# Transformer block with patch tokens, attention over one big row set and a top-2 mixture of experts: the feed-forward part and the elementwise work around it rebuilt

## The chip, the cores and the metric

The kernel runs on one core of one Trainium2 chip. The metric is device time in microseconds for one execution; lower is better. The core has a matrix engine (TensorE, PE in the profile, whose weight loads are PEld), a vector engine (VectorE, DVE), a scalar engine (ScalarE, ACT), a third elementwise engine (GpSimd, POOL) and a queue engine for transfers (SyncE, SP). Matmul results land in PSUM, eight banks of 128 x 512 fp32; GpSimd works on SBUF alone.

## The reference

Input `x` is (8, 64, 128, 64) fp32: batch, channels, time, variables. Each of 8 x 64 series is cut into 16 patches of 16 steps, Fourier-transformed and projected to 64 features, which gives 8192 tokens of 64 features. Then:

```python
f = l2norm(h)                                  # 8192 x 64
attn = softmax(f @ f.T)                        # 8192 x 8192
h = layernorm(h + l2norm(0.8 * f + 0.2 * attn @ f))
logits = h @ router_w.T                        # 8 experts, best 2, weights renormalised
out = h
for e in range(8):
    out = out + combine[:, e:e+1] * (gelu(h @ w1[e] + b1[e]) @ w2[e] + b2[e])
result = layernorm(h + out)
```

## The kernel before

Tokens sit 128 to a tile (`NT` = 64 tiles), and eight tiles make a group (`G` = 8, `NG` = 8 groups), kept in `h` as 128 x 64 tiles x 64 features. Every engine runs an order written out by hand; semaphores tie them together, and each engine takes its own instructions strictly in that order.

1. Up to about 86 us, `x` is loaded in eight pieces of 1 MB per half (three slots in `ring`), multiplied by folded weights (`product`, L368, fp32) and transposed into token tiles (`tokens`, L402, fp32 transposes with 64 rows, the two halves of the array in turn).
2. Attention takes 512 steps `s`: 8 blocks of 1024 queries (`QC`) times 64 key tiles. A step is three fp16 products (`scores`, L431), one exponential on ScalarE (L709, with the row sum as accumulator), one subtraction on VectorE that forms the low part of the probabilities (`low_part`, L794), and the products with the values (`high_sums` L446, `low_sums` L459). Meanwhile GpSimd splits the expert weights into three bf16 parts (L273 to L277, into `wp`).
3. In the last query block, `beside(t)` puts work for the first groups between the steps: `attention_tokens` (L469), `attended` (L815, L818), squares and sums, the scaled residual, mean and variance of the first normalisation, `token_transposes` (L481) and the routing of group 0.
4. The feed-forward loop then runs over 8 groups `g`, with eight slots `s` each. A slot is one pair of experts for 512 tokens: `u = 8 * g + s`, with `n = u // 4` the half group and `i = u % 4` the pair of experts. `up(u)` (L509) makes three matmuls of 512 columns, one for each part in `wp`, against fp16 `hT`, whose 128 rows are the high and the low half of the 64 features. ScalarE applies the activation with the bias (L724). `expand(u)` (L569) spreads the routing weights from 16 rows to 128 rows, `weigh` (L912) multiplies the two on VectorE, `down` (L580) adds two experts' products into bank 4 by its column halves in fp32, and three more matmuls (L586) add the bias `b2`. After each half group bank 4 is copied (L732), transposed back by four fp32 transposes (L596), and added to `h` (L918, L919).

In the same slots the engines work for later groups: `attention_tokens(g + 4)`, `attended(g + 3)` and its norm, the first normalisation of `g + 2` (mean L831, centring on GpSimd L288, squares L667, variance L836, power L280, scaling L841, `high_half` L671, low half on GpSimd L304, transposes L481), the routing of `g + 1` (`logits_out` L863, L864 and `route`, fifteen small instructions from L872 to L905 on 128 x 64 values, then `combine_transposes` L500 and `combine_out` L681), and the second normalisation of `g - 1` (mean L831, centring on GpSimd L348, squares L743, variance L836, power L280, scaling on GpSimd L345), whose result goes out by two DMAs. `up(u)` waits for the activation of `u - 2` and `expand(u)` for `weigh(u - 2)`: banks 0 and 1, and banks 2 and 3, take turns.

GpSimd's order in a group (`elementwise(x, y, q, z)` with x = g + 3, y = g + 2, q = g + 1, z = g - 1), which decides what queues behind what: centre y, power for z - 1, power for the norm of x, power for y, exponential of q, low half of y, residual of x, scale z - 1, centre z. Each of these waits for its own semaphore, so a late one holds up all behind it.

## Time and profile before

| | |
|---|---|
| median of 3 runs | 964.14 us (962.71 to 968.96) |
| profiled execution, own time | 968.87 us |
| its span | 967.1 us, 31034 instructions |
| PE busy | 908.5 us (94%) |
| DVE busy | 801.7 us (83%) |
| ACT busy | 646.4 us (67%) |
| POOL busy | 164.4 us (17%) |
| mean granted TensorE clock | 0.984 of full speed |
| DMA | 26.19 MB, mean 27 GB/s |

Busy time is the union of an engine's instructions. A busy matrix engine is not one at its peak, since matmuls overlap. An fp32 matmul that is no transpose stands in the trace as two MATMUL instructions (128 for the 64 in `down` and 128 for the 64 in `product`). The mean duration of an instruction includes its fill and drain, so that two instructions without a dependence start closer together than their durations say.

### The profile page before, as it was taken

To read this page: it belongs to the slowest core of one execution; us is meant where nothing else is said; L and a number is where in the kernel's file an instruction comes from. 1 tells how busy PE (TensorE), PEld (TensorE's weight loads), DVE (VectorE), ACT (ScalarE), POOL (GpSimd) and SP (SyncE) were. 2 spreads that over 40 slices of the span, in tenths; PEclk is the share of its full clock that TensorE was granted. 3 is DMA by queue.
4 is the path that set the end of the run, shared out by engine and by line. 5 is a ranking of instruction groups with operands and counts; after the bars stand their busy time and mean duration, and the time that the engine had idled before them with its cause. 6 is when DMAs were issued, how large, how long until landed. Compare 5 with 4: busy or idle time off the path is not lost.

```text
span 967.1 us, 31034 instructions
## 1 busy us (share of the span) xinstructions
PE 908.5 (94%) x13562; PEld 547.0 (57%) x13562; DVE 801.7 (83%) x923; ACT 646.4 (67%) x1179; POOL 164.4 (17%) x129
## 2 busy tenths in 40 slices
PE   4987799999999999999999999999998799999895
PEld 2433455566866776786678666666654454333231
DVE  6134998898898889889888988888898898999673
ACT  0223768788778878887777888788766665555352
POOL 3043800000000000000000000000024513466433
PEclk9999999999999999999999999999999999999798
DMA  9695400000000000000000000000000000000001
GB/s 301 193 233 113 79 2 2 2 3 3 2 3 3 2 3 2 3 2 3 2 3 2 3 2 2 3 2 3 2 2 2 1 2 2 1 12 12 12 23 33
DMA packets 28486, 26.19 MB, mean 27 GB/s; under 512 B 9552, under 2 KB 26064, under 8 KB 28352
## 3 DMA queue, kind: packets, MB, share of 16 engines
q1 hardware_dynamic: 19408, 14.98, 6.8%
q10 hardware_dynamic: 8496, 8.57, 3.3%
q8 instruction: 107, 1.75, 0.8%
q0 software_dynamic: 448, 0.67, 0.3%
q14 instruction: 27, 0.22, 0.1%
HBM read 17.92 MB, written 2.10 MB: 21 GB/s over the span
## 4 chain that ended last, share of the span: by engine, by line
PE 81%; DVE 9%; DMA 3%; issue 3%; POOL 2%; ACT 1%; SPq 0%; POOLq 0%; ACTq 0%; DVEq 0%
PE ps L431 31%; PE ps L446 22%; PE ps L459 11%; PE ps L368 5%; DVE ring L794 4%; PE ps L509 3%; DMA ring<-in_x_dram 3%; PE ps L580 3%; PE ps L569 2%; POOL stat L280 1%; PE ps L469 1%; DVE ring L912 1%; PE ps L586 1%; ACT combT L681 1%; PE ps L596 1%
## 5 line engine op out<-in xcount | busy, mean ns | idle before, releaser
L794 DVE TENSOR_TENSOR ring<-ring 128x1024 f16<-128x1024 f32 x512 | 614.1, 1248 | 50.1 <-ACT ring L709 49.1
L709 ACT ACTIVATE ring<-ps 128x1024 f32<-128x1024 f32 x512 | 519.2, 1020 | 145.0 <-PE ps L431 144.9
L431 PE MATMUL ps<-big 64*64 64x512 f16 x6144 | 384.9, 377 | 2.8 <-DVE h L774 2.6
L431 PEld LDWEIGHTS ps<-big 64*64 64x64 f16 x6144 | 225.0, 106 | 115.8 <-DVE h L774 3.0
L446 PE MATMUL ps<-ring,fs 64*64 64x512 bf16 x4096 | 285.4, 387 | 1.6 <-ACT ring L709 0.7
L446 PEld LDWEIGHTS ps<-ring,fs 64*64 64x64 f16 x4096 | 151.0, 106 | 79.3 <-issue 5.3
L459 PE MATMUL ps<-ring,fs 64*64 64x512 f16 x2048 | 163.2, 379 | 16.5 <-DVE ring L794 15.9
L280 POOL TENSOR_TENSOR stat<-stat,cst 128x8 f32<-128x8 f32 x24 | 43.4, 1813 | 683.0 <-DVE stat L823 636.3
L459 PEld LDWEIGHTS ps<-ring,fs 64*64 64x64 f16 x2048 | 73.9, 107 | 57.4 <-issue 21.8
L709 ACT ACTIVATION_READ_ACCUMULATOR ring<-ps 128x1 f32 x512 | 101.7, 199 | 0.0
L368 PE MATMUL ps<-ring,weff 128*128 128x512 f32 x128 | 60.5, 628 | 13.3 <-DMA ring<-in_x_dram 12.8
L724 ACT ACTIVATE ring<-ps,b1s 128x512 f32<-128x512 f32 x64 | 43.4, 682 | 31.2 <-PE ps L509 30.2
L912 DVE TENSOR_TENSOR ring<-ring,ps 128x512 f32<-128x512 f32 x64 | 43.7, 683 | 16.8 <-PE ps L569 9.8
L509 PE MATMUL ps<-big,wp 128*128 128x512 f16 x192 | 54.6, 396 | 0.4 <-ACT ring L724 0.4
L368 PEld LDWEIGHTS ps<-ring,weff 128*128 128x128 f32 x128 | 24.8, 200 | 44.6 <-issue 36.5
L774 DVE TENSOR_REDUCE h<-ps 128x512 f32<-128x1024 f32 x8 | 9.7, 1220 | 43.5 <-PE ps L402 43.5
L580 PE MATMUL ps<-ring,w2s 128*64 128x512 f32 x128 | 36.2, 647 | 0.0
L647 ACT ACTIVATE sums<-ps 128x1024 f32<-128x1024 f32 x8 | 8.1, 1023 | 36.4 <-PE ps L368 36.4
L569 PE MATMUL ps<-combT,sel 16*128 16x512 f16 x64 | 25.4, 396 | 3.1 <-ACT combT L681 2.5
L509 PEld LDWEIGHTS ps<-big,wp 128*128 128x128 bf16 x192 | 16.1, 103 | 20.9 <-issue 9.0
L569 PEld LDWEIGHTS ps<-combT,sel 16*128 16x128 f16 x64 | 5.8, 91 | 32.1 <-issue 26.2
L647 ACT ACT_TABLE_LOAD x1 | 1.3, 1283 | 33.7 <-PE ps L368 33.7
(105 smaller groups left out, 455.5 us busy)
## 6 DMA issues: line engine op xcount, KB each, us to landing
ring<-in_x_dram ACTq DMA_DIRECT2D x8, 1024.0 KB, 13.7
ring<-in_x_dram SPq DMA_DIRECT2D x8, 1024.0 KB, 13.8
big<-big SPq DMA_DIRECT2D x16, 128.0 KB, 2.4
out_dram<-h SPq DMA_DIRECT2D x16, 128.0 KB, 2.4
f<-in_L_tok_W_dram SPq DMA_DIRECT2D x1, 288.0 KB, 4.1
xedge<-in_x_dram POOLq DMA_DIRECT2D x2, 128.0 KB, 7.0
wall<-in_L_ffn_w_dram POOLq DMA_DIRECT2D x2, 128.0 KB, 6.9
cst<-consts_dram ACTq DMA_DIRECT2D x1, 144.0 KB, 2.4
```

The lines of the kernel that those rows point to most:

```text
L280: return gt(stat[:, dst, sl(n)], stat[:, src, sl(n)], minus_half, ALU.pow)
L368: return mm(bank(2 * (b % 2) + q).rearrange("p (m v) -> p m v", v=V), weff[:, s, :], xring[:, b % XR, 8 * q:8 * q + 8, s, :], start=(s == ...
L431: last = mm(bank(SLOT_BANK[slot_of(s)] + r)[m:m + 64, :], of_k[r][:, 128 * k + m:128 * k + m + 64], of_q[r][:, q0 + 512 * r:q0 + 512 * r + ...
L446: last = mm(bank(4 + half)[m:m + 64, :], fs[64 * r:64 * r + 64, s % NT, m:m + 64], probs[64 * r:64 * r + 64, s % 8, :].bitcast(BF16)[:, 10 ...
L459: last = mm(bank(4 + half)[64 * e:64 * e + 64, :], fs[64 * r:64 * r + 64, s % NT, 0:64], probs_lo[64 * r:64 * r + 64, s % 8, 512 * half:51 ...
L509: last = mm(bank(u % 2), wp[:, part, 128 * i:128 * i + 128], hT[:, 512 * n:512 * n + 512], start=(part == 0), stop=(part == 2))
L569: mm(bank(2 + u % 2), sel[:, 128 * i:128 * i + 128], combT[:, n // NCH % 2, t0:t0 + 512], start=True, stop=True).then_inc(s_ex, 1)
L580: last = mm(bank(4)[64 * e:64 * e + 64, :], w2s[:, i + e, :], hidc[:, (u + e) % 4, :], start=(i == 0), stop=False, skip_group_check=True)
L709: a(probs[:, s % 8, :], bank(SLOT_BANK[slot_of(s)], 2), ACT.Exp, accum_out=rowsum[:, s:s + 1]).then_inc(s_pr, 1)
L724: a(hid[:, u % 4, :], bank(u % 2), ACT.Gelu, bias=b1s[:, u % 4:u % 4 + 1]).then_inc(s_gelu, 1)
L794: tt(probs_lo[:, s % 8, :], probs[:, s % 8, :], probs[:, s % 8, :].bitcast(BF16)[:, 1:2 * QC:2], ALU.subtract).then_inc(s_lo, 1)
L912: tt(hidc[:, u % 4, :], hid[:, u % 4, :], bank(2 + u % 2), ALU.mult).then_inc(s_hc, 1)
```

## The change

- `up` in fp32: the weights `w1s` are no longer split. `hT` is now fp32 and holds two tiles one over the other (features of the even tile in rows 0 to 63, of the odd tile in rows 64 to 127), 512 columns for a group. One slot pair is now a pair of experts for the whole group (`u = 4 * g + s // 2`), with two fp32 matmuls of 64 rows, one in each row half of the array, into banks 0 and 1.
- `expand` has the same form: two fp16 matmuls of 16 rows, in rows 0 to 15 and 64 to 79, into banks 2 and 3.
- `down` adds the two experts of a pair at once, for the two token halves in the two column halves of bank 4; the bias is one pass of two fp16 matmuls with prepared weights `b2s`.
- `result` is a true fp32 matmul with the matrix identity minus 1/64 (`centre_of`): transposed back and centred at once, once in a group. The mean, the centring and one of the two additions of the second normalisation go.
- Banks are no longer used in turn: `up(u)` waits for both activations of `u - 1`, `expand(u)` for both `weigh` of `u - 1`.
- GpSimd keeps the powers and the last scaling. Its other full passes go to VectorE as eight narrow instructions (128 x 64) with one value per partition: `attended`, `residual`, `normed`. The first normalisation's squares and their sums are eight narrow activations with accumulator. The split of the weights goes; a small split of `b2` runs on VectorE early.
- The constants grow: `sel_f` from 16 to 128 rows (32 to 256 KB), and `cst2` is new (128 x 262 fp32).

```diff
-                for part in range(3):
-                    last = mm(bank(u % 2), wp[:, part, 128 * i:128 * i + 128], hT[:, 512 * n:512 * n + 512],
-                              start=(part == 0), stop=(part == 2))
+                if u >= 1:
+                    pe.wait_ge(s_gelu, 2 * u)
+                for r in range(2):
+                    rows = slice(64 * r, 64 * r + 64)
+                    last = mm(bank(r), w1s[rows, 128 * i:128 * i + 128], hT[rows, BLK * y:BLK * y + BLK],
+                              start=True, stop=True)
...
-                mm(bank(2 + u % 2), sel[:, 128 * i:128 * i + 128], combT[:, n // NCH % 2, t0:t0 + 512],
-                   start=True, stop=True).then_inc(s_ex, 1)
+                if u >= 1:
+                    pe.wait_ge(s_hc, 2 * u)
+                for r in range(2):
+                    rows = slice(64 * r, 64 * r + 2 * E)
+                    last = mm(bank(2 + r), sel[rows, 128 * i:128 * i + 128], combT[rows, y % 2, :], start=True, stop=True)
...
-                for k in range(CH):
-                    last = mm(bank(5)[:, 128 * k:128 * k + 128], yT[:, n % 2, 128 * k:128 * k + 128], ident,
-                              is_transpose=True, start=True, stop=True)
+                for p in range(TP):
+                    last = mm(bank(5)[:, 128 * p:128 * p + 128], yT[:, z % 2, 128 * p:128 * p + 128], centre_of,
+                              start=True, stop=True)
...
             def elementwise(x, y, q, z):
-                if y < NG:
-                    centre(y)
-                if z >= 1:
-                    pool.wait_ge(s_var2, z)
-                    rsqrt(7, 3, z - 1).then_inc(s_rstd2, 1)
                 if x < NG:
                     attention_scale(x)
-                if y < NG:
-                    deviation(y)
                 if q < NG:
                     exponential(q)
                 if y < NG:
-                    low_half(y)
-                if x < NG:
-                    residual(x)
...
+                    deviation(y)
+                if z >= 0:
+                    pool.wait_ge(s_var2, z + 1)
+                    rsqrt(11, 8, z).then_inc(s_rstd2, 1)
+                    pool.wait_ge(s_rstd2, z + 1)
+                    gt(h[:, sl(z), :], h[:, sl(z), :], wide(stat[:, 11, sl(z)]), ALU.mult).then_inc(s_fin, 1)
...
+            def centred_squared(y, j0, j1):
+                if j0 == 0:
+                    act.wait_ge(s_mean, y + 1)
+                for j in range(G * y + j0, G * y + j1):
+                    last = a(sq_h[:, j % G, :], h[:, j, :], ACT.Square, bias=stat[:, 9, j:j + 1],
+                             accum_out=stat[:, 5, j:j + 1])
...
             def attended(x):
                 dve.wait_ge(s_at, x + 1)
-                tt(att, bank(6).rearrange("p (j o) -> p j o", o=D), wide(stat[:, 6, sl(x)], G),
-                   ALU.mult).then_inc(s_att, 1)
-                dve.wait_ge(s_att, x + 1)
-                stt(f[:, sl(x), :], f[:, sl(x), :], 0.8, att, ALU.mult, ALU.add).then_inc(s_g, 1)
+                for k in range(G):
+                    j = G * x + k
+                    last = stt(f[:, j, :], h[:, j, :], stat[:, 6, j:j + 1], bank(6)[:, D * k:D * k + D], ALU.mult, ALU.add)
+                last.then_inc(s_g, 1)
...
+            def residual(x):
                 dve.wait_ge(s_rn, x + 1)
...
+                for j in range(G * x, G * x + G):
+                    last = stt(h[:, j, :], f[:, j, :], stat[:, 1, j:j + 1], h[:, j, :], ALU.mult, ALU.add)
+                last.then_inc(s_res, 1)
...
+            def normed(y):
+                dve.wait_ge(s_rstd, y + 1)
+                tt(stat[:, 9, sl(y)], stat[:, 9, sl(y)], stat[:, 7, sl(y)], ALU.mult).then_inc(s_shift, 1)
+                dve.wait_ge(s_shift, y + 1)
+                for j in range(G * y, G * y + G):
+                    last = ts(h[:, j, :], h[:, j, :], stat[:, 7, j:j + 1], stat[:, 9, j:j + 1], ALU.mult, ALU.add)
+                last.then_inc(s_ln, 1)
```

The new orders of the three engines in the loop, by slot `s` of a group: TensorE does `combine_transposes(g)` and `up` in slot 0, `up` in the even slots, `expand(u)` and `down(u - 1)` in the odd ones, the logits of `g + 1` in slot 1, `result(g - 1)` in slot 3, the transposes of `g + 2` in slot 7. VectorE does `weigh(u, 0)` in the odd slots and `weigh(u - 1, 1)` in the even ones, `attended` in slot 0, the logits and the norm's sum in slot 2, `result_added` in slot 4, `residual` in slot 5, `mean`, `normed` and the last variance in slot 6, the end of the routing in slot 7. ScalarE does one activation in each slot, two narrow squares behind it in slots 0 to 3, and one or two wide passes.

## Rows read from the trace of the kernel before

**Rows 1.** Windows by stage: busy us of each engine with instructions, TensorE clock, DMA share, GB/s

```profile
27.66:31.07 3.41, 3.41 (x9) 1.52 (x8) 0.00 (x0) 0.00 (x0) 0.00 (x0) 1.00 0.00 0
611.00:696.00 85.00, 84.57 (x1537) 55.21 (x1532) 75.85 (x66) 67.66 (x128) 0.00 (x0) 1.00 0.01 3
696.00:804.00 108.00, 98.02 (x1610) 53.15 (x1606) 96.40 (x118) 72.02 (x134) 34.05 (x19) 0.97 0.01 2
861.95:881.07 19.12, 18.23 (x119) 7.75 (x119) 18.10 (x46) 10.57 (x17) 11.91 (x9) 1.00 0.06 15
900.18:922.94 22.76, 22.38 (x103) 6.88 (x103) 14.40 (x38) 9.95 (x16) 8.12 (x6) 0.70 0.05 13
922.94:939.19 16.25, 15.90 (x95) 5.45 (x95) 11.88 (x35) 8.10 (x13) 5.36 (x4) 1.00 0.08 18
939.19:952.60 13.41, 13.06 (x57) 3.95 (x58) 7.05 (x14) 7.93 (x12) 3.72 (x3) 1.00 0.09 20
952.60:967.06 14.46, 3.08 (x15) 0.84 (x15) 4.76 (x11) 1.23 (x2) 6.40 (x5) 0.74 0.16 36
```

**Rows 2.** Chain that ended last, in one feed-forward group: start, us, what

```profile
844.99 0.67 PE ps L509 x3
845.66 0.32 PE ps L569
845.98 1.01 PE ps L580 x4
```

**Rows 3.** Timeline of PE in the load stage: start, us, instructions merged

```profile
51.49 7.13 PE L368 MATMUL ps<-ring,weff 128*128 128x512 f32 x16
58.56 0.71 PE L402 MATMUL ps<-cst,sums 64*128 64x64 f32 x16
```

**Rows 4.** Lines of DVE from 842.85 to 881.07, by form

```profile
L912 DVE TENSOR_TENSOR ring<-ring,ps 128x512 f32<-128x512 f32 x16 | 10.9, 682 | 1.0 <-issue 1.0
L831 DVE TENSOR_REDUCE stat<-h 128x8 f32<-128x512 f32 x4 | 2.7, 674 | 0.0
L919 DVE TENSOR_TENSOR h<-h,ps 128x256 f32<-128x256 f32 x5 | 2.1, 421 | 0.2
```

**Rows 5.** Timeline near 774.8 (DVE) and near 874.3 (POOL beside DVE)

```profile
774.81 0.23 DVE L876 TENSOR_TENSOR rtmp<-cst,rsmall 128x64 f32<-128x64 f32 x1
774.95 1.22 DVE L794 TENSOR_TENSOR ring<-ring 128x1024 f16<-128x1024 f32 x1
...
874.27 1.26 POOL L296 TENSOR_TENSOR h<-h,f 128x512 f32<-128x512 f32 x1
...
874.33 1.29 DVE L888 TENSOR_TENSOR rtmp<-cst,rsmall 128x64 f32<-128x64 f32 x1
```

**Rows 6.** Lines of ACT from 696 to 804, by form

```profile
L709 ACT ACTIVATION_READ_ACCUMULATOR ring<-ps 128x1 f32 x62 | 12.3, 198 | 0.0
L667 ACT ACTIVATE squares<-h 128x512 f32<-128x512 f32 x2 | 1.3, 630 | 6.9 <-POOL h L288 6.9
```

**Rows 7.** Waits from 696 to 804: us in total, times, longest

```profile
PE ps L459 <- DVE ring L794: 9.8, 3, 4.7
...
DVE stat L831 <- POOL h L296: 6.3, 2, 4.0
```

**Rows 8.** Lines of DVE from 696 to 804, by form

```profile
L794 DVE TENSOR_TENSOR ring<-ring 128x1024 f16<-128x1024 f32 x63 | 78.8, 1302 | 1.8 <-ACT ring L709 1.8
```

**Rows 9.** Lines of DVE from 111.35 to 120.71, while GpSimd splits the weights

```profile
L794 DVE TENSOR_TENSOR ring<-ring 128x1024 f16<-128x1024 f32 x6 | 11.5, 1977 | 0.0
```

**Rows 10.** Windows around the last fall of TensorE's clock

```profile
896.00:900.00 4.00, 1.85 (x13) 0.72 (x13) 3.93 (x11) 0.82 (x2) 1.71 (x2) 1.00 0.28 66
901.47:915.12 13.65, 13.65 (x55) 3.70 (x54) 7.13 (x20) 3.99 (x7) 4.96 (x3) 0.50 0.01 1
```

**Rows 11.** Chain that ended last, its end

```profile
957.32 0.70 DVE stat L831
...
958.29 1.05 POOL h L348
```

More of the change, by code:

```diff
@@ L54 @@
 NG = NT // G
-CH = 4
-NCH = G // CH
-WIDE = NPAIR * 128 + E + D
+TP = G // 2
+HID = NPAIR * 128
+BLK = TP * 128
+PARTS = 3
+MASKS = 2 * PARTS
 XR = 3
@@ L82, in constants @@
         for part in range(2):
-            c[part * E + e, CONSTS + 64 * e:CONSTS + 64 * e + 64] = 1.0
+            for n in range(2):
+                c[64 * n + part * E + e, CONSTS + 64 * e:CONSTS + 64 * e + 64] = 1.0
+    at = CONSTS + HID
+    for n in range(2):
+        rows = slice(64 * n, 64 * n + 64)
+        c[rows, at + 64 * n:at + 64 * n + 64] = np.eye(64) - 1.0 / D
+        for part in range(PARTS):
+            first = 64 * n + 2 * E * part
+            c[first:first + 2 * E, at + 128 + PARTS * n + part] = 1.0
+            for row in range(first, first + 2 * E):
+                c[row % E, at + 128 + MASKS + row] = 1.0
     return c
@@ L489, in router_logits @@
                     pe.wait_ge(s_cev, y)
[L490 to L493 removed]
+                for p in range(TP):
+                    last = mm(bank(7)[:, 2 * E * p:2 * E * p + 2 * E], hT[:, BLK * y + 128 * p:BLK * y + 128 * p + 128],
+                              routers[:, :], start=True, stop=True)
                 last.then_inc(s_lg, 1)
@@ new lines, in down @@
+                for n in range(2):
+                    last = mm(bank(4)[64 * n:64 * n + 64, :], w2s[:, i, :], hidc[:, (2 * u + n) % 4, :],
+                              start=(i == 0), stop=False, skip_group_check=True)
+                if i == NPAIR - 1:
+                    for n in range(2):
+                        last = mm(bank(4)[64 * n:64 * n + 64, :], b2s[:, n, :], combT[:, y % 2, :],
+                                  start=False, stop=True, skip_group_check=True)
+                last.then_inc(s_dn, 1)
@@ L770, in _ @@
             then = chained(dve, s_ch[0])
+            dve.wait_ge(s_self, 32)
+            dve.wait_ge(s_b2c, 1)
+            then(cp(b2f[:, 0, :], b2_rows))
+            for part in range(PARTS):
+                then(cp(b2p[:, part, :], b2f[:, part, :]))
+                if part + 1 < PARTS:
+                    then(tt(b2f[:, part + 1, :], b2f[:, part, :], b2p[:, part, :], ALU.subtract))
+            for n in range(2):
+                at = PARTS * n
+                then(ts(b2f[:, 3, :], b2p[:, 0, :], part_mask[:, at:at + 1], None, ALU.mult))
+                then(stt(b2f[:, 3, :], b2p[:, 1, :], part_mask[:, at + 1:at + 2], b2f[:, 3, :], ALU.mult, ALU.add))
+                then(stt(b2s[:, n, :], b2p[:, 2, :], part_mask[:, at + 2:at + 3], b2f[:, 3, :], ALU.mult, ALU.add))
+            nc.vector.engine_nop().then_inc(s_b2, 1)
             def tokens_out(i):
@@ L826, in attended_normed @@
                 dve.wait_ge(s_rn, x + 1)
-                tt(f[:, sl(x), :], f[:, sl(x), :], wide(stat[:, 1, sl(x)], G), ALU.mult).then_inc(s_gn, 1)
-            def mean(n, ready, done):
-                dve.wait_ge(*ready)
-                then(red(stat[:, 5, sl(n)], h[:, sl(n), :], AX.X, ALU.add))
-                ts(stat[:, 2, sl(n)], stat[:, 5, sl(n)], 1.0 / D, None, ALU.mult).then_inc(done, 1)
-            def variance(n, squares, ready, done):
-                dve.wait_ge(*ready)
-                then(red(stat[:, 5, sl(n)], squares, AX.X, ALU.add))
-                ts(stat[:, 3, sl(n)], stat[:, 5, sl(n)], 1.0 / D, 1e-5, ALU.mult, ALU.add).then_inc(done, 1)
@@ L935, in beside @@
                         attended_squares(i)
+                    if at == 5:
+                        residual(i)
                     if at == 6:
-                        mean(i, (s_res, i + 1), s_mean)
-                    if at == 9 and i < EARLY - 1:
-                        variance(i, sq_h, (s_hsq, i + 1), s_var)
+                        mean(i)
+                    if at == 11 and i < EARLY - 1:
+                        variance(i)
+                    if at == 13 and i < EARLY - 1:
+                        normed(i)
                     if at >= 17 and i == 0:
@@ L992, in _ @@
+                    if s == 4 and z >= 0:
+                        result_added(z)
+                    if s == 5 and x < NG:
+                        residual(x)
+                    if s == 6 and x < NG:
+                        mean(x)
+                    if s == 6 and y < NG:
+                        normed(y)
+                    if s == 6 and z >= 0:
+                        final_variance(z)
                     for step in steps[2]:
```

336 lines of the change are left out of this document (145 added, 191 removed).

## The prediction

> **What bounds the kernel now.** I read four views, in this order.
>
> First the windows by stage [rows 1]. Away from its ends attention is bound by TensorE: from 611 to 696 us it is busy 84.57 of 85 us at full clock, VectorE 75.85. The change doesn't touch that, so some 570 us stay as they are. The last query block with its side work takes 108 us from 696 to 804, against 85 for a plain one. A steady feed-forward group takes 19.12 us, with TensorE busy 18.23 and VectorE 18.10: both are full. Group 5 takes 22.76 at a mean clock of 0.70, group 6 16.25, group 7 13.41, and 14.46 us follow with TensorE nearly idle.
>
> Second the chain of waits inside a group [rows 2]: it runs along TensorE, 0.67 us for the three matmuls of `up`, 0.32 for `expand`, 1.01 for `down`; near a group's end it passes over VectorE's routing, and so both engines must get faster for the group to shorten.
>
> Third VectorE's lines and timeline [rows 4, 5]. Its wide instructions cost 0.68 us. A 128 x 64 instruction lasts 0.23, but the next independent one starts 0.14 us after it. And the same kind of instruction takes 1.29 us when it starts beside a full GpSimd pass of 1.26 us [rows 5]: an instruction with two SBUF inputs waits for GpSimd. `weigh`, with one input in PSUM, keeps its 0.682 [rows 4].
>
> Fourth the waits and lines of the last query block [rows 7, 8]: VectorE waits 6.3 us for GpSimd's residual, TensorE then 9.8 us for VectorE's low parts, and `low_part` lasts 1.302 us in the mean.
>
> **The load stage and the start of attention.** The constants grow by about 0.36 MB. They queue behind three loads of ScalarE's queue, and the DMA share is then 0.00 with TensorE busy on its first products [rows 1] (the window from 27.66 to 31.07), so I take nothing; without that gap it would be a bit over 1 us. The waits for them stand before the third piece's products, and the split of `b2` is 12 small chained instructions on VectorE, about 12 x 0.25 = 3 us, under products of 7.13 us [rows 3]: nothing. Removed is GpSimd's split of the weights: in its 9.36 us six low parts take 11.5 us, 1.977 each [rows 9]. Without it TensorE's own pace of 1.33 us a step (85 / 64) [rows 1] would need 8.0 us for six. I take **-3.5 us** (0 to -5).
>
> **The last query block.** Removed: VectorE's wait of 6.3 us for the residual, ScalarE's of 6.9 us for the centring [rows 6, 7], which holds the exponentials queued behind it, and the conflicts, (1.302 - 1.22) x 63 = 5.1 us [rows 8]. Added on VectorE: three `residual` of 8 x 0.14 = 1.1 us, two `normed` of 8 x 0.14 + 0.2 = 1.3, minus two sums of 0.7 that go to ScalarE's accumulators: +4.5 us in all, or +8 if a narrow instruction costs its whole 0.23. The new waits (`residual` for the power, two steps later in `t`; `normed` for another) stand one step behind small GpSimd work and should be met; if not, `low_part` queues behind them, and then TensorE. What is late next is TensorE: 85 us and some 11 us of side products. With imperfect overlap I put the block at 99.5 instead of 108: **-8.5 us** (-4 to -11).
>
> **A steady feed-forward group, TensorE.** `up` goes from 8 x 0.67 to 4 times two fp32 matmuls. No row has an fp32 product of 64 rows in row halves. A full one costs 7.13 / 8 = 0.89 us (sixteen instructions are eight matmuls) [rows 3]. From below, `down` does two of them in 1.01 us because they lie in column halves [rows 2]; and 16 fp32 transposes of 64 rows, in turn in the row halves, take 0.71 us, 0.033 from one to the next [rows 3], about the time in which 64 columns stream at two cycles each in both halves at once. From above, one after the other, it is 1.9 us. I take 1.0, as in `down`, the nearest row: 4.0 instead of 5.4. `expand`: 4 x 0.32 (at most 4 x 0.55) instead of 8 x 0.32, -1.3. The bias is one pair of matmuls in the column halves instead of six, at 0.3 a pair by `expand`'s row about -0.8 with its switches. The rest (tokens, `down`, logits, transposes back, now true fp32 products but half as many) I take as even, within 0.5 either way. Sum 18.2 - 3.5 = **14.7 us** of TensorE.
>
> **The same group, VectorE.** Removed: one mean (0.68 + 0.17 + gaps, 0.95), one sum for a variance (0.7), the two wide multiplications L827 and L841 (0.68 less the 0.08 by which the next one starts earlier, 0.6 each), the wide pair of `attended` (1.3), four additions of 0.42 (1.7) [rows 4], 5.9 together; and the conflicts with GpSimd, 1.29 - 0.23 = 1.1 for one instruction [rows 5] and as a guess 0.7 for the others, since one full pass of GpSimd stays. Added: 24 narrow instructions at 0.14 = 3.4 (at most 0.23 each, 5.5), the shift 0.2, one wide addition 0.6, wider copies of the routing 0.3, together 4.5. 18.1 - 5.9 - 1.8 + 4.5 = **14.9 us** (14 to 17).
>
> Here a rule speaks against the change: the Trainium skill, VectorE: DVE Perf Modes, section "The TRN2 errata", says that each instruction pays a fixed 58 cycles from SBUF and 120 from PSUM at 0.96 GHz, so that work should be cut no finer than 512 elements. By it eight narrow instructions cost 1.0 us from SBUF and 1.5 from PSUM; an estimate from that page for VectorE's group would be 15.2 us. For SBUF the trace agrees (0.14 us).
>
> **The new waits in a group.** Both banks of `up` belong to one `u`, so `up(u + 1)` waits for both activations: 1.0 + 2 x 0.65 + narrow squares with accumulators (four at 0.3 to 0.45; the accumulator's own row is 0.198 [rows 6]), 2.4 to 3.5 us a pair, under the 4.3 that a group of 17.4 us allows. Behind the waiting `up` on TensorE stand `expand` and `down`, and for them waits `weigh`. At a group's start VectorE has the last `weigh` and `attended`, 1.8 us, to cover transposes, copy, `up` and the first activation, 2.4 us: idle 0.6. In slots 1 to 4 the activations come late behind the squares and the logits; I count 1.9 us more. So 14.9 + 2.5 = **17.4 us** against 19.1, with TensorE idle for nearly 2 us before the routing is ready.
>
> **Sum of the loop.** Groups 0 to 4: -1.6 x 5 = -8.1. Group 5 at full clock, without the attention work: TensorE 12.9 and waits 1.6, 14.5 against 22.76: -8.3. Group 6: 13.7 against 16.25, -2.5. Group 7: four pairs of 1.0 + 0.3 + 1.0 + waits, 11.6 against 13.41, -1.8. The end: mean, its scaling and the centring go, 0.70 + 0.18 + 1.05 + handovers [rows 11], and true products for transposes add 0.4: -2.0. Loop **-22.7 us**.
>
> **Clock.** I have then taken away every stretch of half clock in this part, and that is too much. The clock fell to 1.2 GHz at 901 after TensorE had been busy 1.85 of 4 us, waiting for the routing [rows 10]; it stayed there 13.65 us although TensorE was busy throughout. The new group leaves TensorE more idle, just before each group's start. The price of such a stretch: group 5 took 22.76 with less work than group 4's 19.1 and more than group 6's 16.25 [rows 1], so 4 to 6 us, 5. I take one and a half of them, **+7.5**.
>
> Total: -3.5 - 8.5 - 22.7 + 7.5 = -27.2. The profiled execution took 968.87 us (span 967.1), so it would be 941.7; the three runs' median is 4.7 lower. I forecast **938 us**, its own range 925 to 947.
>
> **Rivals.**
> (a) The half clock becomes the loop's state; this one ends on the other side. Place: the end of each group, where TensorE waits for `combine_transposes`. At half clock a group's matmuls need 2 x 12.5 = 25 us plus handovers, 26 against 17.4, and 22 against 13 to 14.5 in the last ones, so that the whole loop costs +50: 975 to 990. The sign turns when about seven stretches of 13.65 us come (35 us of gain / 5), two thirds of the loop. For it: fp32 streams and frequent small waits, and the 13.65 us in which a busy TensorE didn't regain its clock [rows 10]. Against it: full clock in the other groups with idle gaps in each. The Trainium skill, TensorE: Matmul & The Clock Gate, section "A second HAM failure mode: psum-queue depth-cycling", describes such an oscillation from micro-idles between groups of matmuls. Chance 0.10. In between, three to five stretches: 945 to 957, middle 950, chance 0.14.
> (b) The change doesn't do what it says: the two row halves don't run together in fp32. Then `up` costs +0.9 x 4 = 3.5 a group, TensorE 18.2, groups 0 to 4 about as before (+8), the others +2.5 each: 938 + 15.5 = 953.5. Against it the transposes of rows 3. Chance 0.13.
> (c) Narrow instructions cost their whole 0.23: +2.1 a group on five groups and +3.5 in the query block, and less hidden waiting: 952. For it only the durations, against it the start 0.14 later [rows 5]. Chance 0.08.
> (d) No stretch of half clock and all bounds good: 920. Chance 0.07.
>
> **How the numbers follow.** Forecast 0.48. A measurement here can't tell 1% (9.6 us) from no change, so faster means under 954.5 and slower over 973.8. Faster: 0.48 + 0.07 + 0.12 + 0.07 + 0.06 = 0.80. Same: the rest of (b), (c) and the middle case, and a slow edge of (a), 0.10. Slower: 0.10. The range runs from 920, case (d), to 966, leaving out (a) and little more.
>
> **What the profile would show.** Two fp32 matmuls of `up` in about 1.05 us (1.9 if (b)); `expand` pairs in 0.4; no VectorE instruction of 64 columns over 0.3 us except beside the one GpSimd scaling; steady groups of 17.4 us with VectorE busy near 15; the last query block near 99.5 us, without a wait for GpSimd; low parts at 1.22 us between 111 and 121; 12.5 us after the last activation work; one or two new stretches of half clock. The forecast fails if TensorE's clock stays low in the loop, if starts of VectorE's narrow instructions are 0.23 apart, or if waits for activations leave VectorE idle for over 4 us a group.

## The result: 984.65 us, 1.9% slower

| | before | after |
|---|---|---|
| median | 964.82 us (4 runs, 962.71 to 968.96) | 984.65 us (4 runs, 976.41 to 989.47) |
| ratio to before | | 1.0189, 95% interval 1.0153 to 1.0226 |
| profiled execution, span | 968.87, 967.1 us | 989.47, 987.6 us |
| mean granted clock | 0.984 | 0.947 |

The forecast was 938 (920 to 966), so the time lies outside its range and on the other side. Three marks in both timelines cut the difference of the spans, 20.5 us: VectorE's copy of the sums of query block 6 starts at 700.78 us instead of 698.86 (+1.9); from there to the load of ScalarE's table for the activation it takes 103.28 us instead of 107.75 (-4.5); from there to the end 183.5 instead of 160.5 (+23.0). The loss lies in the feed-forward loop. The four runs of the kernel after scatter by 13 us, in the order of their mean clock: 976.41 us at 0.965, 981.81 at 0.961, 987.49 at 0.950 and 989.47, the profiled one, at 0.947.

Windows of the kernel after, one for the last query block and one for each group (from one `combine_out` to the next; columns as in [rows 1]: start:end, length, busy us of PE, PEld, DVE, ACT, POOL with instructions, granted clock, DMA share, GB/s):

```profile
698.60:801.00 102.40, 95.98 (x1560) 51.17 (x1556) 96.45 (x182) 73.36 (x162) 12.61 (x6) 0.98 0.01 2
804.06:826.27 22.21, 20.10 (x74) 8.40 (x75) 17.11 (x60) 10.09 (x28) 4.91 (x3) 0.62 0.00 0
826.27:848.72 22.45, 18.18 (x84) 8.31 (x84) 14.78 (x51) 10.40 (x29) 6.79 (x5) 0.85 0.00 1
848.72:870.21 21.49, 17.22 (x84) 7.48 (x84) 16.73 (x62) 10.40 (x30) 7.80 (x6) 0.91 0.06 13
870.21:896.66 26.45, 22.40 (x84) 9.70 (x85) 16.30 (x59) 10.40 (x30) 7.37 (x6) 0.69 0.05 11
896.66:917.90 21.24, 15.38 (x68) 5.68 (x68) 16.62 (x60) 10.40 (x30) 7.80 (x6) 0.83 0.05 12
917.90:941.99 24.09, 20.29 (x68) 7.71 (x68) 11.98 (x39) 9.88 (x29) 5.95 (x5) 0.64 0.05 12
941.99:963.23 21.24, 19.54 (x64) 7.17 (x64) 9.73 (x29) 6.66 (x11) 4.14 (x4) 0.62 0.06 13
963.23:987.60 24.37, 13.42 (x64) 4.63 (x64) 8.34 (x15) 7.88 (x13) 6.16 (x5) 0.89 0.14 33
```

Two things are to be seen, and they must be kept apart. The clock column is under 1 in every group; before, of the groups shown, one had less than full clock [rows 1]. And in the group with the best clock, 848.72 to 870.21 at 0.91, no engine is full: TensorE 17.22 of 21.49 us, VectorE 16.73. So the group is too long even apart from the clock: 3.5 us of half clock can cost it at most 1.75 us, which leaves 19.7.

Windows of the kernel after around one fall of the clock:

```profile
866.31:869.56 3.25, 0.66 (x4) 0.42 (x5) 3.15 (x12) 0.60 (x1) 1.53 (x1) 1.00 0.00 0
869.60:886.70 17.10, 15.71 (x47) 6.37 (x47) 8.19 (x27) 6.76 (x23) 6.02 (x5) 0.50 0.07 17
```

TensorE was busy 0.66 of 3.25 us, then its granted clock is 0.50, which is 1.2 GHz, for 17.10 us, although it is busy 15.71 of these. The chain of waits of the kernel after says what it waited for (start, us, what):

```profile
861.71 1.66 DVE h L829 x8
...
864.42 0.56 DVE stat L834
...
865.28 1.87 DVE h L846 x8
867.15 0.60 DVE stat L851
...
868.86 0.26 DVE comb L914
869.12 0.02 issue
869.14 0.37 DVE comb L916
869.51 0.05 issue
869.56 0.61 PE ps L486 x4
870.17 1.15 PE ps L496
```

This answers to [rows 2], where the chain ran along TensorE. From 861.11 to 869.51 us it lies on VectorE: `residual` (L829), the mean (L834), `normed` (L846), the last variance (L851) and the end of the routing (L914, L916) all stand in slots 5 to 7 of its order, and the transposes (L486) that start the next group wait for the last of them. In slots 0 to 4 it is the other way round: ScalarE has the squares and the result's copy, and VectorE waits. The clock falls seven times in the loop (windows of half a microsecond). Four of the falls (849, 869.5, 897 and 941 us) come with a wait of 1.7 us for L916. The others have another wait before them: 1.33 us for the first activation of group 0 (808), 1.61 us in slot 3 for ScalarE's copy of the result, L673 (832), and 1.48 and 1.50 us for `weigh` and `normed` in slots 5 to 7 (914).

Waits of the kernel after from 804 to 988 us, columns as in [rows 7], with the total first:

```profile
ACT ring L679 <- PE ps L496: 68.1, 31, 5.5
...
DVE ring L924 <- ACT ring L679: 30.6, 28, 2.8
...
DVE h L928 <- PE ps L580: 14.4, 8, 3.2
```

The load stage. Windows of both kernels from 5 to 10 us, before first (the last number is GB/s):

```profile
5.00:10.00 5.00, 4.04 (x72) 3.85 (x72) 0.84 (x1) 0.00 (x0) 5.00 (x9) 1.00 1.10 323
```

```profile
5.00:10.00 5.00, 4.10 (x72) 3.94 (x72) 0.58 (x1) 0.00 (x0) 5.00 (x9) 1.00 1.11 250
```

The DMA engines are as busy and move less, though the large loads are the same. The first products start at 19.55 us instead of 15.70, attention's first scores at 95.8 instead of 89.4. Of these 6.4 us, up to 2.7 are the clock again: the sixteen instructions of the seventh piece take 9.84 us (from 75.59) instead of 7.13, with half clock from 74 to 81 us, beginning in a wait of 3.46 us for the loads. The first query block then gives 4.5 us back: from the first scores to its sums' copy 95.1 instead of 99.6.

### The profile page after: what moved, and what is told of

Its sections match the earlier page's. It is cut to its first block, busy times and chain, and to the rows that moved or that the text cites. A ratio compares the mean times of both kernels' runs of the same rounds, so it can differ in the third digit from the quotient of the medians.

```text
span 987.6 us, 30617 instructions
## 1 busy us (share of the span) xinstructions
PE 913.5 (92%) x13276; PEld 538.7 (55%) x13276; DVE 788.4 (80%) x1060; ACT 645.3 (65%) x1283; POOL 107.7 (11%) x87
## 4 chain that ended last, share of the span: by engine, by line
PE 82%; DVE 8%; DMA 4%; ACT 2%; issue 2%; POOL 0%; SPq 0%; ACTq 0%; POOLq 0%; DVEq 0%
PE ps L417 32%; PE ps L432 22%; PE ps L445 11%; PE ps L350 4%; PE ps L496 4%; DMA ring<-in_x_dram 4%; PE ps L567 3%; DVE ring L795 2%; PE ps L455 1%; PE ps L580 1%; DVE h L829 1%; PE ps L478 1%; DVE h L846 1%; PE ps L556 1%; DVE ring L924 1%
## 5 line engine op out<-in xcount | busy, mean ns | idle before, releaser
L795 DVE TENSOR_TENSOR ring<-ring 128x1024 f16<-128x1024 f32 x512 | 605.3, 1231 | 50.6 <-ACT ring L705 49.8
L417 PEld LDWEIGHTS ps<-big 64*64 64x64 f16 x6144 | 217.3, 106 | 127.5 <-ACT ring L705 8.5
L432 PEld LDWEIGHTS ps<-ring,fs 64*64 64x64 f16 x4096 | 146.1, 106 | 83.7 <-issue 4.8
L445 PEld LDWEIGHTS ps<-ring,fs 64*64 64x64 f16 x2048 | 71.7, 107 | 48.6 <-issue 10.4
L350 PE MATMUL ps<-ring,weff 128*128 128x512 f32 x128 | 63.1, 650 | 16.5 <-DMA ring<-in_x_dram 16.0
L567 PE MATMUL ps<-ring,w2s 128*64 128x512 f32 x128 | 45.0, 789 | 10.1 <-ACT ring L673 9.3
L496 PE MATMUL ps<-big,w1s 64*128 64x512 f32 x128 | 49.0, 851 | 1.4 <-ACT ring L679 1.3
L455 PEld LDWEIGHTS ps<-cst,sums 128*128 128x128 f32 x128 | 17.4, 207 | 18.8 <-issue 18.8
L654 ACT ACTIVATE squares<-h,stat 128x64 f32<-128x64 f32 x64 | 21.4, 339 | 5.9 <-DVE stat L835 5.9
L800 DVE COPY sums<-ps 128x1024 f32<-128x1024 f32 x8 | 9.8, 1225 | 15.4 <-PE ps L445 15.4
```

The costliest lines, as they stand in the source:

```text
L350: return mm(bank(2 * (b % 2) + q).rearrange("p (m v) -> p m v", v=V), weff[:, s, :], xring[:, b % XR, 8 * q:8 * q + 8, s, :], start=(s == ...
L417: last = mm(bank(SLOT_BANK[slot_of(s)] + r)[m:m + 64, :], of_k[r][:, 128 * k + m:128 * k + m + 64], of_q[r][:, q0 + 512 * r:q0 + 512 * r + ...
L432: last = mm(bank(4 + half)[m:m + 64, :], fs[64 * r:64 * r + 64, s % NT, m:m + 64], probs[64 * r:64 * r + 64, s % 8, :].bitcast(BF16)[:, 10 ...
L445: last = mm(bank(4 + half)[64 * e:64 * e + 64, :], fs[64 * r:64 * r + 64, s % NT, 0:64], probs_lo[64 * r:64 * r + 64, s % 8, 512 * half:51 ...
L455: last = mm(bank(6)[:, D * k:D * k + D], outT[:, 128 * (G * x + k):128 * (G * x + k) + 128], both, start=True, stop=True)
L496: last = mm(bank(r), w1s[rows, 128 * i:128 * i + 128], hT[rows, BLK * y:BLK * y + BLK], start=True, stop=True)
```

## The experiments

Medians stand against runs of the kernel before on the same chip (964.75, 965.81, 964.65 and 965.65 us in the four sets).

**1. Keep TensorE busy through its waits.** e1 adds fp16 matmuls without use, into the free bank 5, at the places where it idles.

```diff
+            def filler(n, z):
+                if z >= 1:
+                    pe.wait_ge(s_z, z)
+                for _ in range(n):
+                    mm(bank(5), ident16[:, :], sel[:, :], start=True, stop=True)
...
                     if s == 0 and 1 <= g < NG:
+                        filler(7, g - 1)
                         combine_transposes(g)
...
+                    if s == 3 and g < NG:
+                        filler(6, g - 1)
...
+                    if s >= 5 and 4 <= g < NG:
+                        filler(3, g)
...
                     if s == 7 and g + 2 < NG:
+                        filler(4, g)
                         token_transposes(g + 2)
```

> Theory 1 (the half clock): the changed kernel's feed-forward loop spends 85 of its 180 us at 1.2 GHz, because TensorE waits for the end of VectorE's work in each group. Filler matmuls (fp16, 128 x 128 by 512 columns, into bank 5 while nobody reads it) in the places where TensorE waits keep the clock up: mean clock over 0.98, a middle group 19.5 to 20.5 us instead of 21.2 to 26.5, the whole 960 to 967 us. Theory 2 (the order of waits: one pair of banks, and VectorE's work bunched in slots 5 to 7): the clock costs little, since the group waits for VectorE and ScalarE anyway; groups stay over 21 us at full clock and the whole stays 978 to 988 us.

Measured: 964.91 us (10 runs), ratio 1.0004 (0.9993 to 1.0015), mean clock 0.99. Windows of e1, two middle groups:

```profile
840.88:860.54 19.66, 19.18 (x101) 8.62 (x101) 16.41 (x60) 10.40 (x29) 7.59 (x6) 1.00 0.06 14
860.54:880.20 19.66, 19.18 (x101) 8.62 (x101) 16.41 (x60) 10.41 (x29) 7.58 (x6) 1.00 0.06 15
```

More work on TensorE, and 20 us less: from the table load to the end 159.8 us instead of 183.5. To hold the clock gives back the whole loss against the kernel before. It isn't the whole miss: at full clock a group takes 19.66 us, not 17.4, and the loop is as long as it was before the change. The fillers don't make this length: the chain from 841 to 861 us has none of them, and from 851.6 to 860.1 it lies on VectorE.

**2. Wide instead of narrow, waits split by halves.** e2 makes `attended`, `residual` and `normed` two wide VectorE instructions each; e3 lets each half of `up` and `expand` wait for its own bank.

```diff
-                for j in range(G * x, G * x + G):
-                    last = stt(h[:, j, :], f[:, j, :], stat[:, 1, j:j + 1], h[:, j, :], ALU.mult, ALU.add)
-                last.then_inc(s_res, 1)
+                then(tt(f[:, sl(x), :], f[:, sl(x), :], wide(stat[:, 1, sl(x)], G), ALU.mult))
+                tt(h[:, sl(x), :], h[:, sl(x), :], f[:, sl(x), :], ALU.add).then_inc(s_res, 1)
...
                 for r in range(2):
+                    if u >= 1:
+                        pe.wait_ge(s_gelu, 2 * u + r - 1)
```

> attended, residual and normed as two wide instructions (128 x 512) each instead of eight narrow ones of 128 x 64, which the trace shows 0.20 to 0.23 us apart. By these rows a wide pair costs 1.2 to 1.35 us against 1.62, 1.66 and 1.87: 1.3 us less a group on VectorE, all of it in the part of the group where TensorE waits. Theory that the narrow instructions are the loss: 8 to 10 us faster than the changed kernel. Theory 1 (clock): less idle time of TensorE lowers the number of half-clock stretches too, 5 to 20 us faster. Theory that they are hidden: no difference from 976 to 989 us.

> The waits for banks 0 to 3 split by half: each matmul of up waits for the activation of its own bank and each has its own signal, so that the first half of the next pair runs beside the second activation. The two row halves then run less together (0.9 us each on TensorE instead of 1.06 for both). Theory 2 (single pair of banks): in slots 0 to 4, where up and activation take turns, about 0.6 us less a pair, 2 us a group, 10 to 16 us in all. Theory 1: TensorE is busy for longer and idles less, so fewer stretches of half clock as well. If neither holds, the halves lose their overlap and the kernel gets slower by up to 0.8 us a pair, 25 us.

Measured: e2 980.08 us, ratio 1.0160 (1.0143 to 1.0177), clock 0.955; e3 979.26, 1.0157 (1.0138 to 1.0176), clock 0.957. Both are somewhat under the change's 984.65, and their groups 1 to 5 still scatter between 18.8 and 26.4 us, with half clock in most. While the clock swings, the whole times don't tell what the instructions themselves cost. One group of e2 had its clock (the second, 821.13 to 840.17, at 0.99): 19.04 us, against 19.66 in e1.

**3. Move VectorE's work.** e4 moves `residual` from slot 5 to slot 3 and `mean` from slot 6 to slot 4.

```diff
-                    if s == 5 and x < NG:
+                    if s == 3 and x < NG:
                         residual(x)
-                    if s == 6 and x < NG:
+                    if s == 4 and x < NG:
                         mean(x)
```

> residual from slot 5 to slot 3 and mean from slot 6 to slot 4 on VectorE. In slots 0 to 4 VectorE is idle some 4 us a group waiting for activations, in slots 5 to 7 it is full and TensorE waits for it. Theory 2: 1 to 2 us less a group, 5 to 10 us in all. If the work only pushes the later weigh back: no change.

Measured: 960.28 us (one run), span 958.5. Windows of e4, one group:

```profile
845.70:866.10 20.40, 18.05 (x82) 8.38 (x82) 16.28 (x60) 10.39 (x30) 7.55 (x6) 0.83 0.06 13
```

Two calls moved give 29 us of the profiled span (the kernel after was profiled in its slowest run; to its median it is 24), and the chain in the middle groups now lies on TensorE and ScalarE alone. Each middle group still has one stretch of some 6.5 us at half clock. It doesn't begin at the routing's wait, which is gone, but 6 us later, in slot 3, after TensorE has waited 1.61 us for ScalarE's copy. The chain of e4 at such a place, the last line at half clock:

```profile
865.98 0.76 ACT squares L654 x4
866.74 0.49 ACT ring L673
867.23 0.04 issue
867.27 1.98 PE ps L567 x4
```

So there were two places in each group, and the new order of VectorE's work repairs one.

**4. Both together.** e5 is e4 with fillers of 5, 2, 4 and 3 (in slot 3, before the token transposes of slot 7, before `combine_transposes`, and in slots 5 to 7 of the last groups); e6 has the wide instructions in addition, e7 those and the split waits (with a first filler of 4).

> Filler matmuls (fewer: 5, 2, 4 and 3 in a place) and residual and mean in slots 3 and 4. The single run of the earlier residual showed groups of 20.4 us with 6.8 us each at half clock, from which at full clock 18.3 us should be left. If the clock and the bunching of VectorE's work are separate costs: groups of 18.3, the whole 950 to 954 us. If one only hides the other: 958 to 962 us, as the earlier residual alone.

> The same with wide instructions for attended, residual and normed. If the group is bound by VectorE's narrow instructions: another 1.3 us a group, 8 us less than with filler and earlier residual alone. If it is now bound by TensorE with ScalarE's activations in turn, as the chain of the earlier residual says: less than 3 us.

> The same with the waits for banks 0 to 3 split by half. If the single pair of banks is what holds the group at full clock: 1 to 2 us less a group, 8 to 15 us in all. If the halves lose their overlap: up to 0.8 us more a pair.

Measured: e5 954.62 us, ratio 0.9883 (0.9853 to 0.9913), clock 0.994; e6 953.89, 0.988 (0.9846 to 0.9915), e7 954.23, 0.988 (0.9831 to 0.9929). All three have middle groups of 17.9 us. Here wide instructions and split waits bring nothing to a group. The chains of e5 and e6 say why for the wide ones: they lie on TensorE and hold six fillers, 0.43 and 0.86 us (e5):

```profile
873.08 0.43 PE ps L588 x2
873.51 0.44 PE ps L467 x4
873.95 0.86 PE ps L588 x4
```

The query block got 1.5 us shorter by them (101.86 us in e6, 103.36 in e5), but the profiled e6 lost that and more in group 0, which has 10.5 us of half clock and takes 22.46 us instead of 18.08.

**5. The same filler in the kernel before.** Was its own half clock [rows 10] a loss of the same kind? e8 adds three fillers in slots 6 and 7 of the last groups and five ahead of `combine_transposes`.

```diff
+            def filler(n):
+                pe.wait_ge(s_att, NG)
+                for _ in range(n):
+                    mm(bank(6), ident16[:, :], hT[:, 0:512], start=True, stop=True)
...
+                    if s >= 6 and 4 <= g < NG:
+                        filler(3)
```

> The kernel before the change with filler matmuls in groups 4 to 7 (into bank 6, which nobody uses there). It shows what one stretch of half clock of 13.65 us costs there: by the forecast 4 to 6 us, so 959 to 961 us, with group 5 at 17 to 18 us instead of 22.76. If the filler itself costs as much as the clock gives back: 964 to 966 us.

Measured: 968.87 us (10 runs), ratio 1.0035 (1.0017 to 1.0054). No half clock is left in its groups; group 5 takes 19.14 us instead of 22.76, but group 6, which had full clock before, 18.7 instead of 16.25, so that nothing is gained: the eleven fillers of a group cost 2.4 us there. What the stretch itself costs, a later run shows. e10 (experiment 6) is the kernel before with 24 unused bytes, and its profiled execution has no half clock in this group:

```profile
907.03:924.01 16.98, 16.39 (x103) 5.89 (x103) 14.00 (x38) 10.06 (x15) 8.12 (x6) 1.00 0.07 17
```

16.98 instead of 22.76: one stretch costs 5.8 us, and the forecast's price of 5 was about right. Whether fewer fillers than e8's would win it, no run shows. The 23.7 us of e1 are a loss of another size, and the change brought it.

**6. The load stage.** The new tile `cst2` has 262 columns, 1048 bytes per partition, and lies ahead of `ring`, so that the slots for `x` move by 1048 bytes, 24 more than a multiple of 256. e9 makes the tile 1280 bytes wide; e10 puts 24 bytes into the kernel before.

```diff
-        cst2 = sb("cst2", [128, LATE_CONSTS], F32)
+        cst2 = sb("cst2", [128, 320], F32)[:, 0:LATE_CONSTS]
```

```diff
+        gap = sb("gap", [128, 6], F32)
         weff = sb("weff", [128, HALF, 128], F32)
```

> The changed kernel with the new constants' tile cst2 made 320 columns wide instead of 262, so that all tiles behind it, the slots for x in ring among them, lie a multiple of 256 bytes further on than in the kernel before and not 24 bytes off; nothing else differs. Theory A (the place of the slots in SBUF slowed the loads of x): the window from 5 to 10 us moves about 320 GB/s instead of 250, SyncE's issue of its three loads takes 9 us instead of 12.8, attention's first scores start at 88 to 90 us instead of 95.8, and the whole time is about 6 us lower, 978. Theory B (something else in the new start: the two more or larger transfers, GpSimd's memset or its other small loads): 250 GB/s, 12.8 us and 95.8 us stay, and the time is 984.

> The kernel before with an unused tile of 24 bytes per partition ahead of weff and ring, the reverse of the run before. Theory A (place in SBUF): 250 GB/s from 5 to 10 us, first scores at 94 to 96 us instead of 89.4, and some 5 us slower, 970. Theory B: 320 GB/s, 89.4 and 965 as before.

Measured: e9 978.22 us, ratio 1.0147 (1.0087 to 1.0207), against 1.0189 of the change; e10 970.1 us against 964.65, ratio 1.0044 (1.0019 to 1.0069). Windows from 5 to 10 us, e9 first, then e10:

```profile
5.00:10.00 5.00, 4.11 (x72) 3.95 (x72) 0.73 (x1) 0.00 (x0) 5.00 (x9) 1.00 1.05 282
```

```profile
5.00:10.00 5.00, 4.06 (x72) 3.87 (x72) 0.82 (x1) 0.00 (x0) 5.00 (x9) 1.00 1.08 233
```

Attention's first scores start at 89.9 us in e9 (95.8 in the changed kernel) and at 96.3 in e10 (89.4 before): 24 bytes per partition cost 6 to 7 us in these pairs. The intervals of e9 and of the change overlap, that of e10 is clear of 1. All profiles together give a smaller mean: in the eight kernels with the change and without the pad (the change and e1 to e7) the first scores start at 93.7 to 96.8 us, mean 94.9, with 250 to 285 GB/s in this window; in the five with it (e9, e11 to e14) at 89.3 to 91.8, mean 90.4, with 282 to 319; before and e8 at 89.4 and 88.0, with 323 and 315. So the place costs some 4.5 us, and the larger constants at most 1 to 2. The Trainium skill, DMA: Bandwidth & Descriptors, section "How a descriptor splits into AXI transactions", says that a descriptor that doesn't start on a 256-byte boundary fetches bytes that it doesn't use; it speaks of reads, while here the place of the written side moved. Our runs show the price of 24 bytes, not which boundary it is.

**7. What is left at full clock.** e11 is e5 with the padded tile, with a `beside(t)` in which `residual` and all that follows for a group come one step later, and with ScalarE's result copy ahead of its narrow squares. e12 has fewer fillers (5, 1, 3, 2).

```diff
-                    if at == 5:
+                    if at == 6:
                         residual(i)
-                    if at == 6:
+                    if at == 7:
                         mean(i)
```

> Three edits on the kernel with fillers and early residual: the padded cst2; in the last query block the residual of a group one step later and its mean, squares, variance, scaling and transposes with it, so that attended of the next group and residual of this one no longer stand in one step; ScalarE's copy of the result ahead of its narrow squares in slot 2. Theory (VectorE's bunching in one step, 1.57 + 1.42 us beside two low parts, cost the query block its gain): the block from the sums' copy to the last exponential takes 94 to 96 us instead of 98; groups 17.5 instead of 17.9; with 6 us from the load stage, if it was the place in SBUF, 944. Rival (TensorE's own side work fills the block: 96 of 102 us busy): 98 us stay, and 948; without the load stage's gain 6 us more in each case.

> The run before with fewer fillers on TensorE (5 instead of 5 in slot 3, 1 instead of 2 before the transposes of slot 7, 3 instead of 4 before the routing's transposes, 2 instead of 3 in slots 5 to 7 of the last groups). If the fillers on the chain only cost their time, 0.4 us a group less, 940. If the clock needs them, stretches of half clock come back in the loop, and it is 945 to 955.

Measured: e11 947.0 us, ratio 0.9806 (0.9765 to 0.9848); e12 948.24, 0.9811 (0.977 to 0.9852). Sums' copy to table load takes 101.26 and 101.21 us instead of 103.28, 2 us less where I had expected 2 to 4. The groups stay at 17.9 in both, whether TensorE has many fillers or few. The chain of e12 in such a group:

```profile
859.76 1.45 DVE h L842 x7
...
862.42 0.59 DVE h L941
863.01 0.61 DVE stat L847
...
865.91 1.88 DVE h L859 x8
867.78 0.60 DVE stat L864
```

L842 and L859 are `residual` and `normed`: the chain is VectorE's again, and it is long because it is full of narrow instructions. e13 is e12 with the wide instructions of e2, e14 the same with fillers of 4, 0, 2 and 1.

> The last kernel but one (padded cst2, early residual, respaced query block, lighter fillers) with attended, residual and normed of each group as two wide VectorE instructions each. Theory C (VectorE's 24 narrow instructions, 0.20 to 0.23 us apart, set the group of 17.9 us at full clock): VectorE's busy time in a group falls from 16.1 to 15.2 or less, the chain leaves VectorE, a group takes 17.1 to 17.3, the query block one to two us less, and the time is 943. Rival (TensorE's own work and its waits for ScalarE set it): 17.9 us stays, 947.

> The same with still fewer fillers on TensorE: 4 in slot 3, none before the token transposes of slot 7, 2 before the routing's transposes, 1 in slots 5 to 7 of the last groups. If they still hold the clock, groups near 16.7 and 939; if not, stretches of half clock in the middle groups, and 945 to 955.

Measured: e13 941.49 us, ratio 0.9747 (0.9716 to 0.9778); e14 941.5, 0.9740 (0.9707 to 0.9773). A group of e12, then the same group of e13:

```profile
852.71:870.62 17.91, 17.09 (x93) 7.88 (x93) 16.14 (x60) 10.41 (x29) 7.59 (x6) 1.00 0.07 16
```

```profile
846.97:864.18 17.21, 17.08 (x93) 7.88 (x93) 15.67 (x42) 10.41 (x29) 7.58 (x6) 1.00 0.07 17
```

TensorE has the same 17.08 us, and the group is 0.7 shorter, as in all four of the groups 1 to 4; the query block is 2.1 us shorter (99.13). Twenty-four narrow instructions cost VectorE more than six wide ones. e14's middle groups take 17.2 us with 16.5 us of TensorE at full clock, so six fillers a group hold the clock there once VectorE's order is right, and TensorE isn't the bound: the chain runs over ScalarE's squares, a power of 1.65 us on GpSimd and VectorE. In group 0 they don't hold it: e14 has 10 us of half clock there and takes 20.91 us, e13 17.52. Both kernels are the fastest versions here, 2.5% under the kernel before.

## Why the prediction was wrong, point by point

**What was right.** The two row halves run together in fp32, and with that rival (b) falls. Timeline of PE in the kernel after at full clock:

```profile
862.53 1.13 PE L496 MATMUL ps<-big,w1s 64*128 64x512 f32 x4
...
864.32 0.39 PE L556 MATMUL ps<-combT,sel 16*128 16x512 f16 x2
```

Four instructions, two products, 1.13 us (1.06 in the chain of e4), where 1.0 was taken; the `expand` pair 0.39, where at most 0.55 was allowed. (The transposes of [rows 3] pointed there, but not at two cycles a column: 64 columns so, in both halves at once, would be 0.027 us, and the row has 0.033. The better comparison is the kernel before's fp32 transposes of 128 columns over all rows: four take 0.67 us and one 0.27, so they start 0.13 apart, and half the columns would be twice 0.033.) Low parts last 1.221 us in the last block instead of 1.302 [rows 8], and the split's removal gave 4.5 us in the first block, for the 3.5 (0 to 5) of the load stage's term. From the last `combine_out` to the end it takes 24.4 us; the forecast's terms for group 7 and the end made 24.1.

**The clock, +7.5: the step that failed most, and the one that turned the sign.** The price of a stretch, 5 us, was right (5.8); the number of stretches was not. Measured in its place: e1's full clock is worth 23.7 us of the loop, net of its fillers. I counted one and a half stretches of half clock, because the kernel before had one. The trace after has five of over 6 us between 808 and 958 us, and two of 3.5. The row for it was in the prediction: TensorE busy 1.85 of 4 us and then 13.65 us at half clock in spite of full work [rows 10]. Rival (a) named the place, the wait ahead of `combine_transposes`, and the sign, and its 975 to 990 holds the time, but not by its own price: it had +50 for the clock (its items, 8.6 us in each of five groups and 8 to 10 in each later one, add up to nearly 70), of which 23.7 came, and the rest is the length of the groups. That its range holds the time is luck in part. By the number of stretches it was the case in between, three to five (0.14); its 945 to 957 lacks the longer groups. Rival (a) got 0.10. What should have raised it: the prediction says itself that TensorE idles nearly 2 us at this place in each group, so the cause came seven times and not one and a half; four falls followed it, and three followed waits that no rival named. The Trainium skill's description of this oscillation (TensorE: Matmul & The Clock Gate, "A second HAM failure mode: psum-queue depth-cycling") puts it down to frequent micro-idles between groups of matmuls; the 17.10 us above agree in kind, but the idle time before them is a wait of 1.69 us and one of 0.91.

**The steady group, 17.4: the second failure.** Measured 19.66 at full clock in e1, and the larger part of it is the order, not the sum of the work. I added up VectorE's work (14.9) and waits (2.5), and never laid it out along the slots: after moving two pieces forward, e5 takes 17.9. From the table load to the end that is 149.8 us instead of e1's 159.8, the 10 us that this step missed. The sums were mis-sized too: VectorE is busy 16.4 us in e1 for 14.9, TensorE 15.40 in e2's group at 0.99 for 14.7. The timeline of VectorE in the last query block of the kernel after has the narrow instructions:

```profile
724.63 1.65 DVE L829 SCALAR_TENSOR_TENSOR h<-f,stat,h 128x64 f32<-128x64 f32 x8
...
726.77 1.62 DVE L818 SCALAR_TENSOR_TENSOR f<-h,stat,ps 128x64 f32<-128x64 f32 x8
```

Eight take 1.65 and 1.62 us, 0.20 us from one to the next, and `normed`'s eight 1.87, 0.23. I had taken the 0.14 of [rows 5], from an instruction that has no value per partition. The operation isn't what differs: in the kernel before a `SCALAR_TENSOR_TENSOR` of this size with a constant in place of the value starts at 865.46 us, and the next instruction at 865.60. So rival (c), with 0.08, was nearly true, with 0.20 and 0.23 for its 0.23: 24 x 0.07 is 1.7 us of VectorE a group. The Trainium skill's advice to cut no finer than 512 elements (VectorE: DVE Perf Modes, section "The TRN2 errata") is borne out by e13, 17.21 us a group for 17.91. The estimate from that page's fixed cost, 1.0 us for eight from SBUF, is too low against the 1.65 to 1.87 here.

**The last query block, -8.5: got -4.5.** The wait of VectorE for GpSimd and TensorE's for the low parts are gone, as forecast. What is late next was read wrong: `residual(i)` and `attended(i + 1)` fall into one step (`at` 5 and 0, with starts 5 apart), 1.57 + 1.42 us on the chain near 724 and 743 us, and the low parts behind them wait, and TensorE for these. One step later gives 2.0 us (e11), wide instructions 2.1 more (e13), which is the forecast.

**The load stage, -3.5: got +1.9.** The split's part was right; "the constants cost nothing" was wrong, for a reason that no row showed: less by their bytes than by the place to which they push `ring` (e9, e10).

**Sum of the misses** against 941.7 for the profiled execution: load stage 5.4, query block 4.0, loop 38.2, in all 47.6 of 47.8 us. Of the loop's 38.2, the clock is 16.2 (23.7 for 7.5). The other 22.0 are the groups at full clock: 10.0 for VectorE's bunching (e1 to e5, which has six fillers fewer in a group), 5.7 for the narrow instructions (e11 to e13, with the lighter fillers in it); some 6 us are left in e13. Its groups show where: group 0 takes 17.52 us, where the forecast had taken 1.6 from 17.4 (in the kernel before this group never took 19.1); group 5 takes 16.46 for 14.5, group 6 15.53 for 13.7, the rest 25.1 for 24.1; groups 1 to 4 take 17.2 for 17.4. What makes them long, fillers among other things, isn't separated. Two slips in the prediction's sums are small beside this: five groups at 19.12 less 17.4 are 8.6 us and not 8.1, and 941.7 less 4.7 is 937 and not 938.

**Open.** That TensorE's waits bring the falls is shown by the fillers, and by e4, in which shorter waits left less half clock. How short a wait is harmless isn't shown (1.61 us was not, in e4); nor whether fp32 products in place of fp16 ones make the clock fall sooner.

## What to carry to other kernels

When a change makes every engine lighter, the group isn't as long as the fullest engine: write the new order of each engine along the slots and look for the slot in which the work of one engine stands ahead of the wait that starts the next group. If that wait comes once in each group, price the clock once for each group, and look for a second wait that takes over when the first is gone. A few useless matmuls in the gaps tell on the chip whether it is the clock, but they cost time of their own where TensorE is full (e8). Give a new tile a width that leaves the tiles behind it where they were, before you read anything into a slower load.

## What the runs showed of the hardware

- TensorE's clock fell to 1.2 GHz after 0.66 us of work in 3.25 us and stayed there 17.10 us with 15.71 us of work. With 6 (e14) to 17 (e1) fp16 matmuls of filling in a middle group it stayed at 2.4 GHz, and e1 became 20 us faster by doing more. One stretch of 13.65 us cost a group of the kernel before 5.8 us (22.76 against 16.98 in e10).
- 24 bytes per partition in the place of a load's target changed 323 into 233 GB/s at the start (e10) and moved attention by 7.0 us; over all profiles with the change the mean shift is 4.5 us.
- A VectorE instruction of 128 x 64 with a value per partition starts 0.20 us (three inputs) or 0.23 us (two values) after the one before, one without such a value 0.14 us, also of the three-input kind. ScalarE's narrow square with accumulator takes 0.34 us, as `beside` and the loop of the kernel after have it eight times a group:

```profile
857.62 0.34 ACT L654 ACTIVATE squares<-h,stat 128x64 f32<-128x64 f32 x1
857.86 0.19 ACT L654 ACTIVATION_READ_ACCUMULATOR squares<-h,stat 128x1 f32 x1
```

- Two fp32 products of 64 rows and 512 columns in the two row halves take 1.06 to 1.13 us together at full clock and, in the chain of e4, 2.01 at half.
